# One row of small TensorE work per pair in layer 0, and x turned into the keys' banks

## The reference

```python
xn = layer_norm(x, norm_w, norm_b)
q = (xn @ q_w + q_b).reshape(Bx, Tx, H, -1)          # H = 16 heads
k = (xn @ k_w + k_b).reshape(Bx, Tx, H, -1)
att = softmax(einsum('bnhl,bmhl->bnmh', q, k) + mask, axis=2)
v = ((xn @ v_w + v_b) * src_mask[:, :, None]).reshape(Bx, Tx, H, -1)
y = einsum('bnmh,bmhl->bnhl', att, v).reshape(Bx, Tx, Dx)
h = layer_norm(y, sb_norm_w, sb_norm_b) * (1.0 + scale) + shift   # scale, shift from the condition
return x + silu(h) @ out_w + out_b
```

## Time and profile before

| | us |
|---|---|
| runs shown (median of 3) | 1049.34 (1049.16 to 1050.51) |
| profiled execution | 1049.48 |
| its span, first to last instruction | 1047.7 |
| PE busy | 1025.5 (98%) |
| DVE busy | 771.5 (74%) |
| ACT busy | 610.0 (58%) |
| POOL busy | 577.1 (55%) |

### The profile page before, as it was taken

How to read it: one execution, slowest core, us unless ns; L and a number is a source line. 1 busy time by engine, 2 the same in 40 slices (tenths; PEclk the granted TensorE clock), 3 DMA queues, 4 the chain that set the end, 5 groups by cost and what they waited for, 6 DMA issues and landing times. The chain is left out here.

```text
span 1047.7 us, 26078 instructions
## 1 busy us (share of the span) xinstructions
PE 1025.5 (98%) x8572; PEld 891.5 (85%) x8572; DVE 771.5 (74%) x1352; ACT 610.0 (58%) x2021; POOL 577.1 (55%) x864
## 2 busy tenths in 40 slices
PE   8899999999999999999999999999999999999997
PEld 7579888988889888988887778888888888888886
DVE  7646866687666766677669787778778877777876
ACT  6357676876778676776777454433434444443353
POOL 2245456655565456555466565666556555566632
PEclk9999999999999999999999999999999999999999
DMA  9752111211112111221113211122221111112101
GB/s 307 242 184 67 35 56 43 65 55 33 58 49 65 43 45 45 63 58 38 59 50 117 91 56 57 56 67 65 65 65 57 38 55 62 54 60 65 45 31 51
DMA packets 46119, 73.74 MB, mean 70 GB/s; under 512 B 8275, under 2 KB 14547, under 8 KB 46069
## 3 DMA queue, kind: packets, MB, share of 16 engines
q1 hardware_dynamic: 46066, 73.11, 21.9%
q10 hardware_dynamic: 2, 0.00, 0.0%
HBM read 56.28 MB, written 16.81 MB: 70 GB/s over the span
## 5 line engine op out<-in xcount | busy, mean ns | idle before, releaser
L682 ACT ACTIVATE prob<-prob,neg_max 128x128 f32<-128x128 f32 x512 | 198.6, 395 | 78.2 <-DVE neg_max L983 78.2
L1366 PE MATMUL bank<-xt_hi,w_hi 128*128 128x256 f32 x752 | 213.9, 284 | 0.0
L483 POOL TENSOR_SCALAR stat<-stat 128x1 f32<-128x1 f32 x128 | 35.5, 277 | 320.5 <-DVE stat L944 292.8
L1367 PE MATMUL bank<-xt_lo,w_hi 128*128 128x256 f32 x752 | 209.6, 279 | 0.0
L1368 PE MATMUL bank<-xt_hi,w_lo 128*128 128x256 f32 x752 | 209.5, 279 | 0.0
L1366 PE MATMUL bank<-w_hi,xt_hi 128*128 128x512 f32 x384 | 157.7, 411 | 0.0
L1368 PE MATMUL bank<-w_hi,xt_lo 128*128 128x512 f32 x384 | 151.4, 394 | 0.0
L1367 PE MATMUL bank<-w_lo,xt_hi 128*128 128x512 f32 x384 | 150.4, 392 | 0.0
L1367 PEld LDWEIGHTS bank<-xt_lo,w_hi 128*128 128x128 f32 x752 | 142.0, 189 | 1.3
L1366 PEld LDWEIGHTS bank<-xt_hi,w_hi 128*128 128x128 f32 x752 | 141.4, 188 | 1.4 <-DVE z_a L1027 0.2
L1368 PEld LDWEIGHTS bank<-xt_hi,w_lo 128*128 128x128 f32 x752 | 141.9, 189 | 0.0
(11 more groups left out here) (132 smaller groups left out, 2338.4 us busy)
## 6 DMA issues: line engine op xcount, KB each, us to landing
x_in<-in_x_dram SPq DMA_DIRECT2D x32, 256.0 KB, 2.7
x_res<-in_x_dram SPq DMA_DIRECT2D x32, 256.0 KB, 2.6
between_layers<-x_res SPq DMA_DIRECT2D x32, 256.0 KB, 2.0
x_in<-between_layers SPq DMA_DIRECT2D x32, 256.0 KB, 3.3
x_res<-between_layers SPq DMA_DIRECT2D x28, 256.0 KB, 2.6
out_dram<-x_res SPq DMA_DIRECT2D x28, 256.0 KB, 2.0
room<-in_L_cond_W_emb_dram SPq DMA_DIRECT2D x8, 512.0 KB, 6.3
prob<-in_L_cond_emb_w_dram SPq DMA_DIRECT2D x4, 512.0 KB, 12.0
```

Source lines behind the costliest of these rows:

```text
L483: pool.tensor_scalar(v[:, 8:9], v[:, 7:8], EPS, None, ALU.add).then_inc(s[a_in].sem, 1)
L682: last = act.activation(prob[:, b, i, :], prob[:, b, i, :], ACT.Exp, bias=neg_max[:, b, i:i + 1], accum_out=row_sum[:, b, h:h + 1])
L1366: pe.matmul(o, a_hi, b_hi, start=start, stop=False)
L1367: pe.matmul(o, a_hi, b_lo, start=False, stop=False)
```

## The change

On PE, in `step0`: the values of the first sequence come in one piece of 12 matmuls; then, in a row, the last probabilities, both turned x, the second `weigh`, the first `turn_yn`, the second `y_rows`. x is turned into banks 0 and 1, the keys' banks, in place of 5 and 4. ACT takes `xt_high(n, 0)` ahead of `y_t_out(k, 1)` and `xt_high(n, 1)` ahead of `tanh(k, 0)`. DVE takes `xt_low(n, 0)` ahead of `film_scale(k, 0)` and `xt_low(n, 1)` ahead of `y_norm(k, 1)`; both stood behind `s_low_part(k, 0)`. No instruction is added or removed.

```diff
-        FIRST = dict(X=(5, 4), PT=(4, 5), Q=(6, 7), K=(0, 1), V=(3, 6), PV=(7, 7), Y=(2, 2), H=(6, 7), O=(5, 6))
+        FIRST = dict(X=(0, 1), PT=(4, 5), Q=(6, 7), K=(0, 1), V=(3, 6), PV=(7, 7), Y=(2, 2), H=(6, 7), O=(5, 6))
...
+                xt_high(n, 1 - slot, 0, FIRST)
                 y_t_out(k, 1)
+                xt_high(n, 1 - slot, 1, FIRST)
                 if i == 0:
                     act.wait_ge(mask_saved, 32)
                 tanh(k, 0)
-                xt_high(n, 1 - slot, 0, FIRST)
-                xt_high(n, 1 - slot, 1, FIRST)
                 s_high(k, 0)
...
+                xt_low(n, 1 - slot, 0, FIRST)
                 film_scale(k, 0)
                 if i == 0:
                     film(1, 2)
                 if i == G - 2:
                     low_part(1, WK, (0, 1))
                 silu(k, 0)
+                xt_low(n, 1 - slot, 1, FIRST)
                 y_norm(0, k, 1 - slot, 1)
                 s_low_part(k, 0)
-                xt_low(n, 1 - slot, 0, FIRST)
-                xt_low(n, 1 - slot, 1, FIRST)
                 v_add(0, FIRST, f, slot, 1)
...
-                values(0, FIRST, f, slot, 0, range(C - 1))
+                values(0, FIRST, f, slot, 0)
                 if i == 0:
                     embed(1, range(4, KE), 6, EMB_SUMS[2])
                 turn_probs(k, 1, (2, 3))
-                values(0, FIRST, f, slot, 0, (C - 1,))
+                turn(n, 0, FIRST)
+                turn(n, 1, FIRST)
+                weigh(k, 1 - slot, 1)
                 turn_yn(0, k, 0)
                 if i == 0:
                     film(1, 2)
-                weigh(k, 1 - slot, 1)
-                turn(n, 0, FIRST)
-                turn(n, 1, FIRST)
                 y_rows(k, 1)
                 values(0, FIRST, f, slot, 1)
```

## The result

The changed kernel takes **1077.28 us** (median of 4 runs, 1075.49 to 1077.69) against 1049.25 of the kernel before, run beside it. The ratio is 1.0263, with a 95% interval of 1.0249 to 1.0277. The forecast was 1073.9 in a range of 1065 to 1084. The profiled execution took 1077.26 us, its span is 1075.5 us, and the mean granted clock is 0.997.

What follows compares the result with a forecast made beforehand. PE, 98% busy, was taken to bound the kernel, with a slackless chain from film_scale to the output; 1049.48 + 25.9 for fourteen tails - 1.5 for the first step = 1073.9 us, range 1065 to 1084.

Steps and rivals of the forecast that it cites:

- part 1: PE's own time at the step's end: 10.49 us before, 10.47 in the new order, so the row is worth 0.02.
- what bounds the kernel: PE, 98% busy, its matmul order setting the time; one chain without slack from film_scale to the output.
- The second start: The values' last chunk on PE, named beside the first sequence's turned y as where the slackless chain starts.
- part 2: Chain followed from the values' start: turned y at 274.63 instead of 272.58, silu 1.8 us later; 1.85 us a step taken.
- Neutral swap behind silu: DVE does x's second low half first behind silu; the output still follows silu's start by as much, so no cost.
- part 4: Rest of the step, output to next values: stays 22.7 us, no new wait; second y's turn loses 0.61 of margin.
- part 3: PE's waits in the tail: y_rows 0.39, second values 0.13, scores 0.9, output 0.6; net of earlier costs 1.85.
- One tail 1.85, fourteen 25.9: Step tails i = 1 to 14: each pays 1.85 us, together 25.9; that of i = 14 may pay 2.1.
- part 5: The ends: fourteen tails pay 25.9 us; the first step gains between 0 and 2.4, taken as -1.5.
- the third rival: PE's clock falls in the tails amid small works and waits: 24 us, 1098; one tail in four, 1080. Chance 0.12.
- The second rival: Only y_rows' 0.39 and weigh's 0.10 waits are paid, film chain hidden: 3.4 us more, 1052.9. Chance 0.05.
- the first: Rival: only the bank 5 wait goes, the chain having hidden slack: 3.4 us won, 1046.1. Chance 0.05.

Runs made afterwards that it cites:

- row_mended: Changed kernel, PE order probabilities, turned y, first x, weigh, second x, y_rows; film_scale before x's first low half, silu and tanh before its second halves: 1050.69 us, ratio 1.0007.
- yn_late: Kernel before, with only the first turned y moved behind the second weigh on PE: 1065.63 us, ratio 1.0153.
- low_ahead: Changed kernel, with the low half of the second x ahead of silu on DVE: 1068.56 us, ratio 1.0168.
- values_whole: Kernel before, with only the first sequence's values in one piece of 12: 1049.25 us, ratio 0.9991.
- old_banks: Changed kernel, with x turned into banks 5 and 4 as before, all orders kept: 1091.13 us, ratio 1.0393.
- x_early: Kernel before, with the first x's high half ahead of tanh on ACT and low half between film_scale and silu on DVE: 1045.84 us, ratio 0.9957.
- yn_first: Changed kernel, with the first turned y moved directly behind the probabilities, ahead of both x and weigh: 1070.22 us, ratio 1.0191.
- yn_first_film: yn_first, with film_scale ahead of the first x's low half on DVE: 1057.72 us, ratio 1.0074.
- x_early_first: x_early, with the first sequence's values in one piece in the first step alone: 1044.38 us, ratio 0.9946.

## Why the prediction was right, step by step

**That PE's order sets the time, and that the row itself is worth nothing (part 1): right.** row_mended has nearly the whole row, its step is 0.26 above that of before, nearly all of it waits, and it stands at 1.0007 because its first step is 2.0 shorter. PE's own time in the row is worked out at the end of this document: 0.02.

**That one chain without slack runs from the turned y to the output (what bounds the kernel): right, and shown.** yn_late delayed only its start, by 1.36, and silu came 1.32 later; low_ahead shortened only its part behind silu, by 0.61, and the step gave back 0.57. The second start that the prediction names, the values' last chunk, is worth 0.1: in values_whole film_scale no longer stands behind v_add, and silu comes 6.99 behind the values' start instead of 7.10.

**The chain's start (part 2).** Behind the values' start at 279.41, forecast and measured: probabilities 2.75 and 2.75; ACT's copies done 4.53 and 4.54; weigh 4.68 and 4.68; the turned y 5.69 and 5.69. Up to here it is exact. Then film_scale 6.33 and 6.48, add_shift 7.18 and 7.36, silu 8.92 and 9.11, the output 12.6 and 12.71. **The term that was too small is the step from the turned y to film_scale**: I took its record as 0.60, as before, and 0.04 for the handover; it was 0.66 and 0.13. So in this tail silu came 2.01 later, not 1.8. The 0.04 came from another handover (values to v_add), not from this one, which no row of before showed bare because film_scale stood behind v_add there.

**Neutral swap behind silu: right.** The output starts 3.60 behind silu (292.12 - 288.52), forecast 281.50 - 277.86 = 3.64.

**What follows in the step (part 4): right.** From the output to the next values PE takes 22.68 on average over the loop, before 22.73, and it never waits by name for the second turned y.

**The waits (part 3).** Forecast: y_rows 0.39, second values 0.13, scores 0.9, output 0.6. The named ones are 0.21, none, 0.85 and 0.43. By distance the first is the predicted size (y_rows 0.86 behind the y, whose work takes about 0.49: 0.37): a bracket counts from the modelled end of the record, so it shows less than the distance does. The second is named only on the weight loads of the values of the second sequence (fence below); by distance these start 0.67 behind y_rows, 0.35 before, so it is 0.3 where 0.13 was forecast, the lateness of film_scale again. The output stands 1.61 behind the scores, of which 0.51 is wait, where 0.6 was forecast. The sum by distances: weigh 0.10, y_rows 0.37, values 0.31, scores 290.51 - 286.63 - 2.93 = 0.95, output 0.51, together 2.24; less the 0.28 that this place waited before, 1.96. The weight load of those values in after (same columns, PEld is the weight load):

```profile
286.63 0.19 PEld L1366 LDWEIGHTS bank<-w_hi,xt_hi 128*128 128x128 f32 x1 [0.28 <-DVE z_a L1027]
```

**One tail 1.85, fourteen 25.9.** Measured 1.95, and 2.4 in the step of i = 14, for which 2.1 was allowed: together 27.8. This is 1.9 of the 3.4 us by which the forecast was low; the first step is 1.7, and the start and the later program make -0.2.

**The first step (part 5): the step that failed.** Forecast -1.5, measured +0.2. Its structure was right, as PE's timeline of after shows:

```profile
70.00 0.66 PE L1476 MATMUL bank<-ident,yn 128*128 128x128 f32 x4
...
73.27 0.91 PE L1468 MATMUL bank<-ident,y_t 128*128 128x128 f32 x4 [0.90 <-DVE film_ab L936]
```

The wait of 1.38 ahead of the y is gone, and y_rows waits 0.90 for the film (taken as 1.0). What did not go is the slow clock. Two windows of after, both in the first step, the first of them ahead of the changed row (columns as above):

```profile
49.60:53.10 3.50, 3.50 (x12) 0.37 (x8) 0.09 (x1) 0.00 (x0) 1.61 (x2) 0.51 0.36 136
...
73.50:77.00 3.50, 3.50 (x12) 2.82 (x11) 3.20 (x6) 0.63 (x1) 0.53 (x1) 0.51 0.60 229
```

Both have a granted clock of 0.51, that is 1.2 GHz. The second follows the 0.90 wait, and there twelve products took 4.39 us instead of 2.95: 1.4 us that the forecast had counted as won. From the values' start to the next scores the first step is therefore only 0.4 shorter than before (15.9 instead of 16.3). The first window holds part of the embedding sum, whose sixteen matmuls took 5.30 us where before, at full clock, they took 4.70; up to that point the step had already lost 0.6, which the forecast had not in its sum at all. That the 0.90 wait brought the second stretch with it is not shown: old_banks has the same wait of 0.90 at the same place (72.62) and no slow stretch behind it.

**The clock in the loop (the third rival): did not happen.** The two steps shown ran at 1.00, and the two windows above are the only stretches of after at half the clock. By the Trainium skill (TensorE: Matmul & The Clock Gate, Part 4, PE-mode transpose) transposes do not count as a busy PE; with 3.7 us of small work in each tail and waits such as the 0.85 and 0.43 above, no tail of the loop showed a fall, so nothing here made that rule cost anything.

**The rest.** The start cost 0.3 and the later program gave 0.5 back; neither was forecast, and neither was followed further. The second rival (only the small waits, 1052.9) and the first (1046.1) are excluded by 1077.28. The 1046.1 is, however, what x_early reached by another way (1045.84): the wait was real, and its price right by the step (0.23 against 0.245).

## What to carry to other kernels

When TensorE is nearly always busy, look for the one small wait that a step still has and follow it back over the other engines: if each stage starts 0.03 to 0.2 us behind the last, the place of the first TensorE instruction of that chain is dear, and work moved ahead of it is paid for nearly in full (in yn_late 1.36 us later, 1.11 more in the step). To take such a wait away, first move work out from behind the chain's stages on the waiting engines into their idle time (two lines here, 0.4%) before touching TensorE's order. Where an order on one engine was fitted to another's, change both together: yn_first kept one DVE instruction where the changed kernel's order had put it, and moving that one too took back 12.5 of its 20.3 us.

## What the runs showed of the hardware

**The clock in the first step is not a matter of one wait.** In the first step before, the granted clock was at half from about 70.4 to 73.9 us. In the other profiled executions a stretch of 3.5 us began at 48.4 (yn_late), 47.7 (values_whole), 49.6 (yn_first), 47.0 (old_banks), 49.5 (row_mended), twice in after (49.6, 73.5) and in low_ahead (51.2, 75.1); x_early had one from 70.1 to 77.0 and one at 12.1, before its first scores; yn_first_film and x_early_first had none. At 48 us, PE is still ahead of everything that these kernels reorder in the first step. All eleven wait there 1.6 to 3.3 us for the transfer of the embedding weights; seven have a slow stretch at that place and four have none, and the length of the wait does not part them (1.92 in old_banks with one, 2.48 in before without). Near 70 us it is the same: behind the turned y's wait of 1.38 before and x_early are slow, behind a wait of 1.38 for the film (74.73) yn_first is not. With one profile of each it stays open what decides it. A stretch over twelve products cost 1.4 us; one over the embedding sum cost up to 0.6 and in yn_late nothing (4.68 us for its matmuls instead of 4.70). So values_whole and row_mended, which lie that near to 1.0, are to be read by their steps and not by their totals.

**A handover's price depends on the pair of instructions, and not on the engines alone.** From TensorE to DVE it is 0.13 for y to film_scale in the tail of after (and 0.14 in row_mended, 272.71 to 272.85), but 0.04 before for y_rows to y_norm, also four transposes and one DVE instruction (266.37 to 266.41); why is not shown. From DVE to POOL 0.19; from ACT to DVE 0.04 (tanh's end 288.48 to silu 288.52). The six on the way of after from ACT's copies to the output (0.14, 0.13, 0.19, 0.03, 0.04, 0.06) add up to 0.59, about as much as one DVE instruction of this size (0.61).

**Large and small batches on TensorE cost the same.** The values took 2.75 us in one piece (279.41 to 282.16) and 2.07 + 0.78 = 2.85 in two before, change-overs included; against that the small works took 286.63 - 282.16 = 4.47, of which 0.78 are the waits above, 3.69 where it was 0.79 + 0.53 + 1.01 + 0.93 + 0.35 = 3.61. So 0.10 is won, 0.08 lost, and 0.02 remains, as forecast.
